# An audio tower on one core: the first quarter's turning and attention's first six projections, placed inside the convolution's last four iterations

## The chip, the cores and the metric

The kernel runs on one core of a Trainium2 chip. The metric is the device time of one execution in microseconds (us). The core's engines run side by side and meet only in semaphores: TensorE (PE; its weight loads are listed as PEld), VectorE (DVE), ScalarE (ACT), GpSimd (POOL) and SyncE (SP), whose queue issues the DMAs of this kernel. Each engine takes its own instructions in order.

## The reference, cut to what matters

```python
# x: [16, 64, 2048]; the convolution tokenizer makes h: [16, 128, 1024]
h = conv1d(x, conv_in_w, stride=1, pad=3)                       # 64 -> 128 channels, 7 taps
h = gelu(groupnorm1(h, gn1_w, gn1_b))
h = conv1d(h, dw_w, stride=2, pad=2, groups=H) + dw_b           # depthwise, 5 taps
h = conv1d(h, pw_w)                                             # pointwise, 128 -> 128
h = gelu(groupnorm1(h, gn2_w, gn2_b))
# then, each on layernorm(h):
q, k, v = n @ Wq.T, n @ Wk.T, n @ Wv.T     # 32 query heads, 8 key/value heads of 128
q, k = rotate(q), rotate(k)                # rotary position: x*cos + rotate_half(x)*sin
out = softmax(q k^T / sqrt(128)) v         # 4 query heads per key head, rows of one sequence: 128
h = h + out @ Wo.T
# ... routed low-rank experts, autocorrelation by a Fourier transform, a second routed layer
```

The last three stages aren't touched by the change.

## The kernel before

**Convolution** (`conv_stage`). 16 batches go through a software pipeline of 20 iterations, `it` = 0 to 19. In iteration `it` the 7-tap convolution of batch `it` runs on TensorE (48 products of 512 columns in four chunks, `conv`, L502 to L518), its means are taken on VectorE one iteration later (`head(0, it-1)`), the first gelu and the depthwise taps two later (`taps(it-2)`, four instructions on VectorE, L463), the pointwise product three later (`pointwise(it-3)`, L543) with `head(1, it-3)` behind it, and the second gelu, which writes row block `it-4` of `h`, four later (ScalarE, L386). `middle(it)` and `tail(it-1)` on VectorE, with two tiny products `average` on TensorE (L535), turn both means and variances into scale and shift: `tail` is a chain of sixteen small dependent instructions, and its last (L452) releases ScalarE's gelus. The batches end at `it` = 15, so iterations 16 to 19 have no `conv`; `from_end(it)` is 5 for iteration 15, and 4, 3, 2, 1 for the last four.

**Turning the first quarter** (`QuarterRows`). Attention works on quarters of four batches. For the first quarter, VectorE takes statistics of `h` (`rows.stats`, L170) in iterations 16 and 17 and the coefficients (`rows.coefficients`, `keep`, L175 to L183) in iteration 18. ScalarE normalizes (L192) and TensorE transposes (L204) through two PSUM banks; ScalarE rounds the result to `x_hi` (L212) and VectorE takes the rest as `x_lo` (L220). Batch b's transposes wait until batch b-1's `x_lo` has left the banks. All transposes stand in iteration 19.

**Attention** (`attention_stage`). It opens with a block that primes 27 semaphores, then `first()` and a step with `att` false that only makes the projections of the first head group: six tiles j = 0 (key), 1 (value), 2 to 5 (queries). One tile is 24 products of 512 columns (L1014 to L1016: 8 of `w_hi` by `x_hi`, 8 of `w_hi` by `x_lo`, 8 of `w_lo` by `x_hi`). Its weights land in one of two staging buffers; ScalarE makes `w_hi` (`split_w`, L727), VectorE `w_lo` (`low_w`, L885). Key and query tiles are rotated by four VectorE instructions (`rope_out`, L844 to L852), the value tile is copied by ScalarE (`v_out`, L759) and transposed (`turn_v`, L1069). Two PSUM banks alternate between tiles, so tile j waits for the rotation of tile j-2. Then 32 full steps follow, with scores (L1024), exponentials (L743), values and output products (L1061), each beside the next head group's projections.

The weights w_o of the output product are loaded by `load_o`, two tiles in `first()`. `after(engine, sem, n)` waits for a count of n+1 (the priming adds one).

Of the kernel before, what the change touches and what calls it, by code (L numbers as in the profile page):

```python
# [120 lines left out]
VALUES = TILES - 1  # L121

# [15 lines left out]
class QuarterRows:  # L138
# [6 lines left out]
    def __init__(self, nc, ctx, h, ident):  # L145
# [19 lines left out]
        prime(nc, [self.norm, self.normed, self.turned, self.hi_done, self.lo_done])  # L165
# [58 lines left out]
def conv_stage(nc, h, ident, ones_mean, x, conv_w, dw_w, chan, pw_wT, rows, w_stage):  # L224
# [8 lines left out]
    with ExitStack() as ctx:  # L233
# [65 lines left out]
        with nc.Block() as block:  # L299

            @block.sync
            def _(sp_):
# [9 lines left out]
                def body(it, par, on):  # L312
# [43 lines left out]
            def _(act):  # L356
# [16 lines left out]
                def body(it, par, on):  # L373
# [22 lines left out]
                    if from_end(it) == 2:  # L396
                        rows.normalize(act, 0, 0)
                        rows.normalize(act, 0, 1)
                    if from_end(it) == 1:
# [3 lines left out]
                        rows.high(act, 0, cp, 3)  # L403
                    if on(0):
                        evacuate(it, par, 0)
                        evacuate(it, par, 1)
                steps(act, body)

            @block.vector
            def _(dve):  # L410
# [55 lines left out]

                def body(it, par, on):
                    if not early(it, 2):
                        tail(it - 1)
                    if on(1):  # L470
                        head(0, it - 1, [raw[1 - par][:, c // 2, c % 2 * BANK:(c % 2 + 1) * BANK] for c in range(NCH)])
                    if on(3):
                        dve.wait_ge(pw_done, it - 2)
                        head(1, it - 3, [pp[:, c, :] for c in range(2)])
                    if on(2):
                        taps(it - 2, par, (1, 2))
                    if from_end(it) == 4:
                        dve.wait_ge(gelu2, QB)
                        rows.stats(dve, 0, rows_link, 0)
                        rows.stats(dve, 0, rows_link, 1)  # L480
# [4 lines left out]
                    if from_end(it) == 3:  # L485
                        rows.stats(dve, 0, rows_link, 2)
                        rows.stats(dve, 0, rows_link, 3)
                    if from_end(it) == 2:
                        rows.coefficients(dve, rows_link)
                        rows.keep(dve, rows_link, rows.rstd[:, :], rows.shift[:, :])  # L490
# [3 lines left out]
                rows_link = Links(dve, rows.norm, 1)  # L494
                steps(dve, body)

            @block.tensor
            def _(pe):
# [47 lines left out]
                def body(it, par, on):  # L546
# [5 lines left out]
                    if from_end(it) == 1:  # L552
# [9 lines left out]
                steps(pe, body)  # L562


def attention_stage(nc, h, ident, w_o, rope, rows, w_stage, next_rstd, next_shift):
# [8 lines left out]
    ROPED = TILES - 1  # L574
    with ExitStack() as ctx:
        def sb(name, shape, dt=F32):
            return ctx.enter_context(nc.sbuf_tensor(name, shape, dt))

# [3 lines left out]
        def psum(name):  # L582
            return ctx.enter_context(nc.psum_tensor(name, [P, BANK], F32))

        x_hi, x_lo = rows.x_hi, rows.x_lo
        o_stage = [sb(f"at_ostage{i}", [P, L]) for i in range(2)]
# [1716 lines left out]
```

## Time and profile before

| | |
|---|---|
| median of 3 runs | 2864.49 us |
| lowest, highest | 2861.25, 2867.18 us |
| profiled execution | 2863.8 us |
| its span, first to last instruction | 2862.1 us |
| outside the span | 1.7 us |
| mean granted TensorE clock | 0.979 of full |

| span, us | what runs |
|---|---|
| 0 to 240 | setup and iterations 0 to 15 of the convolution |
| 240 to 293 | iterations 16 to 18 |
| 293 to 306 | iteration 19 with the turning |
| 308 to 348 | attention's six projections alone |
| 348 on | 32 attention steps, then the last stages |

The timeline gives start and length of an instruction, or of a run of like ones (x4 is four of them), with the idle time of the engine before it and what ended that in square brackets. A window's granted clock is a share of full speed, 1.00 being 2.4 GHz and 0.50 being 1.2 GHz.

### The profile page before, as it was taken

How to read it: one execution, taken by the hardware profiler on the slowest of the kernel's cores; microseconds unless marked ns; L12 is line 12 of the kernel's file. 1: busy time of each engine (PE TensorE's matmuls, PEld its weight loads, DVE VectorE, ACT ScalarE, POOL GpSimd, SP SyncE). 2: the span in 40 equal slices, each digit the busy share in tenths (PEclk: the TensorE clock that was granted, in tenths of full speed). 3: DMA queues.
4: the chain of work that ended last, by engine and by line, in shares of the span. 5: the costliest groups of instructions: out<-in, count | busy, mean ns of one | idle time of the engine just before them, and what ended most of it. 6: DMA issues, size and time to landing. Idle time of an engine off the chain costs nothing. (4 is left out here: it accounts for less than half of the span.)

```text
span 2862.1 us, 37184 instructions
## 1 busy us (share of the span) xinstructions
PE 2722.3 (95%) x13162; PEld 2265.1 (79%) x13162; DVE 1812.0 (63%) x3247; ACT 980.8 (34%) x2012; POOL 108.2 (4%) x65
## 2 busy tenths in 40 slices
PE   7994799999999999999999999999999997899999
PEld 6773688888878888887888888788888876688888
DVE  4887566666765666667766666776666665872221
ACT  3553333332343333334323333333333333542121
POOL 2110000000000000000000000000000000221110
PEclk9997899999999999999999999999999998999999
DMA  4330232222222232222222222122222224000000
GB/s 111 74 74 0 74 99 91 78 81 81 81 67 82 76 98 90 81 81 74 75 82 81 73 95 95 57 92 81 81 81 74 80 66 155 2 16 30 25 27 30
DMA packets 55327, 206.69 MB, mean 72 GB/s; under 512 B 6769, under 2 KB 7153, under 8 KB 53169
## 3 DMA queue, kind: packets, MB, share of 16 engines
q1 hardware_dynamic: 55216, 205.26, 22.6%
q8 instruction: 64, 1.05, 0.2%
q14 instruction: 47, 0.38, 0.0%
HBM read 196.85 MB, written 8.39 MB: 72 GB/s over the span
## 5 line engine op out<-in xcount | busy, mean ns | idle before, releaser
L1014 PE MATMUL at_proj<-qr_xhi,at_whi 128*128 128x512 f32 x1536 | 614.5, 400 | 12.4 <-DVE at_wlo L885 8.0
L1016 PE MATMUL at_proj<-qr_xhi,at_wlo 128*128 128x512 f32 x1536 | 600.7, 391 | 0.0
L1015 PE MATMUL at_proj<-qr_xlo,at_whi 128*128 128x512 f32 x1536 | 599.0, 390 | 0.0
L755 ACT CAST at_ohi<-at_ov 128x512 fp32r<-128x512 f32 x128 | 75.2, 587 | 846.3 <-PE at_ov L1043 846.3
L1014 PEld LDWEIGHTS at_proj<-qr_xhi,at_whi 128*128 128x128 f32 x1536 | 289.2, 188 | 69.2 <-DVE at_wlo L885 8.7
L1016 PEld LDWEIGHTS at_proj<-qr_xhi,at_wlo 128*128 128x128 f32 x1536 | 288.6, 188 | 63.5
L1015 PEld LDWEIGHTS at_proj<-qr_xlo,at_whi 128*128 128x128 f32 x1536 | 289.6, 189 | 56.3
L1061 PE MATMUL at_out<-at_wohi,at_ohi 128*128 128x512 f32 x1008 | 311.5, 390 | 4.0 <-DVE at_wolo L890 3.0
L1061 PE MATMUL at_out<-at_wolo,at_ohi 128*128 128x512 f32 x1008 | 311.2, 390 | 0.0
L1061 PE MATMUL at_out<-at_wohi,at_olo 128*128 128x512 f32 x1008 | 311.2, 390 | 0.0
L897 DVE TENSOR_TENSOR h<-h,at_out 128x1024 f32 (+1 forms) x126 | 152.9, 1213 | 209.8 <-PE at_out L1061 209.8
L881 DVE TENSOR_TENSOR at_olo<-at_ov,at_ohi 128x512 fp32r<-128x512 f32 x128 | 88.3, 690 | 272.4 <-ACT at_ohi L755 272.4
L885 DVE TENSOR_TENSOR at_wlo<-at_wstage,at_whi 128x1024 fp32r<-128x1024 f32 x192 | 234.3, 1220 | 7.1 <-DMA at_cs<-in_rope_dram 5.4
L1061 PEld LDWEIGHTS at_out<-at_wohi,at_ohi 128*128 128x128 f32 x1008 | 189.7, 188 | 43.9 <-issue 3.3
L1061 PEld LDWEIGHTS at_out<-at_wolo,at_ohi 128*128 128x128 f32 x1008 | 189.8, 188 | 39.6
L1061 PEld LDWEIGHTS at_out<-at_wohi,at_olo 128*128 128x128 f32 x1008 | 189.8, 188 | 39.5
L727 ACT CAST at_whi<-at_wstage 128x1024 fp32r<-128x1024 f32 x192 | 203.0, 1058 | 42.0 <-PE at_proj L1016 39.1
L743 ACT ACTIVATE at_probs<-at_sc,at_ntop 128x128 f32<-128x128 f32 x512 | 181.5, 367 | 102.0 <-DVE at_ntop L859 101.6
L890 DVE TENSOR_TENSOR at_wolo<-at_ostage,at_wohi 128x1024 fp32r<-128x1024 f32 x128 | 153.6, 1221 | 1.4 <-ACT at_wohi L733 1.4
L733 ACT CAST at_wohi<-at_ostage 128x1024 fp32r<-128x1024 f32 x128 | 131.7, 1057 | 36.8 <-DMA at_ostage<-in_w_o_dram 36.5
L844 DVE TENSOR_TENSOR at_q<-at_proj,at_cs 128x512 f32<-128x512 f32 x128 | 88.1, 688 | 84.3 <-PE at_proj L1016 83.8
L1024 PEld LDWEIGHTS at_sc<-at_k,at_q 128*128 128x128 f32 x1024 | 132.0, 192 | 7.9 <-issue 0.6
(245 smaller groups left out, 4066.3 us busy)
## 6 DMA issues: line engine op xcount, KB each, us to landing
at_wstage<-in_w_qkv_dram SPq DMA_DIRECT2D x192, 512.0 KB, 3.7
at_ostage<-in_w_o_dram SPq DMA_DIRECT2D x128, 512.0 KB, 4.4
cv_x<-in_x_dram SPq DMA_DIRECT2D x32, 512.0 KB, 6.5
out_dram<-h SPq DMA_DIRECT2D x16, 512.0 KB, 2.6
fn_w_lo_raw<-in_w_t_dram SPq DMA_DIRECT2D x8, 512.0 KB, 8.6
fn_qka_lo_raw<-in_qka_t_dram SPq DMA_DIRECT2D x5, 512.0 KB, 12.3
fn_w_lo_raw<-in_dft_fwd_dram SPq DMA_DIRECT2D x4, 512.0 KB, 8.1
shared_raw<-in_a_route_dram SPq DMA_DIRECT2D x1, 544.0 KB, 3.9
```

Of the source, the lines that this page charges most:

```text
L727: act.copy(w_hi[j % 2][:, :], w_stage.buffers[j % 2][:, :]).then_inc(whi_done, 1)
L733: act.copy(wo_hi[:, r, :], o_stage[r % 2][:, :]).then_inc(wohi_done, 1)
L743: last = act.activation(probs[:, r, :], sc[b % 2][:, r * P:(r + 1) * P], ACT.Exp, bias=ntop[:, r:r + 1], scale=SCALE, accum_out=total[:, r ...
L881: dve.tensor_tensor(o_lo[:, :], ov[:, :], o_hi[:, :].bitcast(F32), ALU.subtract).then_inc(olo_done, 1)
L885: dve.tensor_tensor(w_lo[j % 2][:, :], w_stage.buffers[j % 2][:, :], w_hi[j % 2][:, :].bitcast(F32), ALU.subtract).then_inc(wlo_done, 1)
L890: dve.tensor_tensor(wo_lo[:, r, :], o_stage[r % 2][:, :], wo_hi[:, r, :].bitcast(F32), ALU.subtract).then_inc(wolo_done, 1)
L897: dve.tensor_tensor(hb, hb, part, ALU.add).then_inc(added, 1)
L1014: pe.matmul(proj[:, j % 2, :], hi[:, w], x_hi[:, k, :], start=(k == 0), stop=False)
L1015: pe.matmul(proj[:, j % 2, :], hi[:, w], x_lo[:, k, :], start=False, stop=False)
L1016: last = pe.matmul(proj[:, j % 2, :], lo[:, w], x_hi[:, k, :], start=False, stop=(k == KT - 1))
L1024: last = pe.matmul(sc[b % 2][:, r * P:(r + 1) * P], qT[par][:, r, cols], kT[par][:, cols], start=True, stop=True)
L1061: last = pe.matmul(banks[:, c, :], a[:, rows], w[:, r, c * BANK:(c + 1) * BANK], start=first, stop=end)
```

## The change

The statistics and coefficients of the first quarter move to the end of iteration 15, with the first two normalizations; the transposes, `high` and `low` move to iteration 16. The six projections with their splits and rotations stand in iterations 16 to 19 between the steps of the convolution, in a class `Projections` that attention also uses; attention loses its opening step. The first two weight tiles are loaded in iteration 0, ahead of the second input; further ones once the convolution's products are done, and the rotation table too. `w_o` is loaded in attention's `first()` as before, which now stands directly ahead of the first full step. The priming of 13 semaphores moves to SyncE's queue in iteration 0: the block of five in `QuarterRows` goes, and attention's block primes 18. `AttentionBuffers` gives attention's buffers the same places in both stages, over the convolution's input buffers.

SyncE's queue:

```diff
+                    if early(it, 1):
+                        for s in rows.sems + pro.sems:
+                            sp_.sem_inc(s, 1)
+                        w_stage.load(sp_, 0, 0)
+                        w_stage.load(sp_, 0, 1)
                 steps(sp_, body)
-                w_stage.load(sp_, 0, 0)
-                w_stage.load(sp_, 0, 1)
+                sp_.wait_ge(xlo_done, NB)
+                sp_.wait_ge(conv_done, NB * NCH)
+                pro.load_rope(sp_, rope)
+                for j in range(TILES + 1):
+                    after(sp_, pro.wlo_done, j + 1)
+                    w_stage.load(sp_, (j + 2) // TILES, (j + 2) % TILES)
```

ScalarE:

```diff
-                    if from_end(it) == 1:
+                    if from_end(it) == 4:
+                        act.wait_ge(xlo_done, NB)
+                        pro.split_w(act, 0, 0)
                         rows.high(act, 0, cp, 0)
                         rows.normalize(act, 0, 2)
...
-                    if from_end(it) == 2:
-                        rows.normalize(act, 0, 0)
-                        rows.normalize(act, 0, 1)
-                    if from_end(it) == 1:
+                    if from_end(it) == 4:
                         rows.high(act, 0, cp, 1)
                         rows.normalize(act, 0, 3)
                         rows.high(act, 0, cp, 2)
                         rows.high(act, 0, cp, 3)
+                        pro.split_w(act, 0, 1)
+                    if from_end(it) == 3:
+                        pro.split_w(act, 0, 2)
+                        pro.split_w(act, 0, 3)
+                    if from_end(it) == 2:
+                        pro.split_w(act, 0, 4)
+                        pro.split_w(act, 0, 5)
+                    if from_end(it) == 1:
+                        pro.split_w(act, 1, 0)
+                        pro.v_out(act, 0)
...
+                    if from_end(it) == 5:
+                        rows.normalize(act, 0, 0)
+                        rows.normalize(act, 0, 1)
```

VectorE:

```diff
+                    if from_end(it) == 5:
+                        dve.wait_ge(gelu2, QB)
+                        link = Links(dve, rows.norm, 1)
                         for b in range(QB):
-                            rows.low(dve, 0, cp, b)
+                            rows.stats(dve, 0, link, b)
+                        rows.coefficients(dve, link)
+                        rows.keep(dve, link, rows.rstd[:, :], rows.shift[:, :])
+
+                def ending(it, par, on):
+
+                    def last_16():
+                        tail(15)
+                        heads(16, 0, on, lambda: rows.low(dve, 0, cp, 0))
+                        dve.wait_ge(conv_done, NB * NCH)
+                        pro.low_w(dve, 0, 0)
+                        taps(14, 0, (1, 2))
+                        rows.low(dve, 0, cp, 1)
+                        middle(16)
+                        rows.low(dve, 0, cp, 2)
+                        rows.low(dve, 0, cp, 3)
+                        taps(14, 0, (3, 4))
+                        pro.low_w(dve, 0, 1)
+
+                    def last_17():
+                        tail(16)
+                        dve.wait_ge(pro.rope_in, 16)
+                        pro.rope_out(dve, 0, 0, 0)
+                        heads(17, 1, on, lambda: None)
+                        taps(15, 1, (1, 2))
+                        pro.low_w(dve, 0, 2)
+                        middle(17)
+                        taps(15, 1, (3, 4))
+                        pro.rope_out(dve, 0, 0, 1)
+                        pro.low_w(dve, 0, 3)
+
+                    def last_18():
+                        tail(17)
+                        pro.rope_out(dve, 0, 0, 2)
+                        pro.low_w(dve, 0, 4)
+                        heads(18, 0, on, lambda: None)
+                        pro.rope_out(dve, 0, 0, 3)
+                        pro.low_w(dve, 0, 5)
+                        middle(18)
+
+                    def last_19():
+                        tail(18)
+                        pro.rope_out(dve, 0, 0, 4)
+                        pro.low_w(dve, 1, 0)
```

TensorE:

```diff
-                    if from_end(it) == 1:
-                        pe.wait_ge(raw_done, NB * 2)
-                        for b in range(QB):
-                            rows.turn(pe, 0, cp, b)
...
+                def ending(it, par, on):
+
+                    def last_16():
+                        pe.wait_ge(raw_done, NB * 2)
+                        rows.turn(pe, 0, cp, 0, 1)
+                        pointwise(13, 1)
+                        average(16, on, 0)
+                        rows.turn(pe, 0, cp, 2)
+                        average(16, on, 1)
+                        rows.turn(pe, 0, cp, 3)
+                        pro.project(pe, 0, 0, 0)
+
+                    def last_17():
+                        pointwise(14, 0)
+                        pro.project(pe, 0, 0, 1)
+                        average(17, on, 0)
+                        average(17, on, 1)
+                        pro.project(pe, 0, 0, 2)
+
+                    def last_18():
+                        pro.project(pe, 0, 0, 3)
+                        pointwise(15, 1)
+                        pro.project(pe, 0, 0, 4)
+                        average(18, on, 0)
+                        average(18, on, 1)
+
+                    def last_19():
+                        pro.project(pe, 0, 0, 5)
+                        pe.wait_ge(gelu2, NB)
+                        pro.turn_v(pe, 0, ident)
```

`attention_stage`:

```diff
             first()
-            step(0, -1, 1, False, 2, False)
...
                 def first():
-                    sp.dma_start(cs[:, :, :], rope).then_inc(rope_in, 16)
                     load_o(0, 0, 0)
                     load_o(0, 0, 1)
-                    after(sp, wlo_done, 1)
-                    w_stage.load(sp, 0, 2)
```

`split_w`, `low_w`, `v_out`, `rope_out`, `project` and `turn_v` of `Projections` hold the same instructions and waits as the functions of `attention_stage` that they replace; `heads` is the two `head` calls with a place between them.

## Rows read from the trace of the kernel before

**Rows 1.** Page of the profile: TensorE's busy time, share of the span, instructions

```profile
PE 2722.3 (95%) x13162; PEld 2265.1 (79%) x13162; DVE 1812.0 (63%) x3247; ACT 980.8 (34%) x2012; POOL 108.2 (4%) x65
```

**Rows 2.** Windows by engine: start:end, length, busy (x) per engine, granted clock, DMA

```profile
238.50:262.00 23.50, 4.70 (x8) 1.97 (x8) 19.26 (x56) 5.24 (x5) 0.00 (x0) 0.64 0.00 0
...
292.00:307.00 15.00, 7.76 (x32) 6.12 (x32) 8.38 (x27) 10.23 (x13) 0.00 (x0) 0.50 0.00 1
```

**Rows 3.** Timeline, start and length in us, VectorE: iteration 16 of the convolution

```profile
240.02 0.16 DVE L447 TENSOR_SCALAR cv_var<-cv_sp 128x2 f32<-128x2 f32 x1
...
243.06 2.46 DVE L424 BATCH_NORM_STATS2 cv_st<-cv_raw 128x6 f32<-128x512 f32 x4
...
248.39 1.29 DVE L424 BATCH_NORM_STATS2 cv_st<-cv_pp 128x6 f32<-128x512 f32 x2 [2.56 <-PE cv_pp L543]
...
252.61 2.88 DVE L170 BATCH_NORM_STATS2 qr_st<-h 128x6 f32<-128x512 f32 x4
...
256.17 2.61 DVE L463 SCALAR_TENSOR_TENSOR cv_y<-cv_g,cv_dww,cv_y 128x1024 f32<-128x1024 f32 x2
```

**Rows 4.** Timeline: the coefficients' first instruction on VectorE, then ScalarE behind their last

```profile
288.57 0.20 DVE L176 BATCH_NORM_AGGREGATE qr_mv<-qr_st 128x2 f32<-128x12 f32 x1
...
292.40 2.37 ACT L192 ACTIVATE qr_xn<-h,qr_shift,qr_rstd 128x1024 f32<-128x1024 f32 x2 [10.51 <-DVE qr_shift L183]
```

**Rows 5.** Timeline, ScalarE and TensorE: iteration 16, with iteration 15's pointwise product first

```profile
230.45 1.95 PE L543 MATMUL cv_pp<-cv_y,cv_pw 128*128 128x512 f32 x4 [0.50 <-ACT h L386]
...
243.18 1.21 ACT L386 ACTIVATE h<-cv_pp,cv_shift,cv_scale 128x1024 f32<-128x1024 f32 x1 [3.90 <-DVE cv_shift L452]
...
244.29 2.08 ACT L391 ACTIVATE cv_g<-cv_raw,cv_shift,cv_scale 128x2048 f32<-128x2048 f32 x1
...
244.53 3.75 PE L543 MATMUL cv_pp<-cv_y,cv_pw 128*128 128x512 f32 x4 [6.18 <-ACT h L386]
```

**Rows 6.** Timeline: the turning stretch, its first instructions and its last

```profile
293.79 1.94 PE L204 MATMUL cv_cp<-ident,qr_xn 128*128 128x128 f32 x8 [4.82 <-ACT qr_xn L192]
...
295.53 0.69 DVE L220 TENSOR_TENSOR qr_xlo<-cv_cp,qr_xhi 128x512 fp32r<-128x512 f32 x1
...
305.11 0.69 DVE L220 TENSOR_TENSOR qr_xlo<-cv_cp,qr_xhi 128x512 fp32r<-128x512 f32 x1 [0.16 <-ACT qr_xhi L212]
```

**Rows 7.** Timeline: attention's start and the first two projections

```profile
307.92 1.99 ACT L727 CAST at_whi<-at_wstage 128x1024 fp32r<-128x1024 f32 x2 [2.85 <-PEq L81]
...
312.50 0.79 PE L1014 MATMUL at_proj<-qr_xhi,at_whi 128*128 128x512 f32 x1 [8.05 <-DVE at_wlo L885]
...
320.18 0.69 DVE L844 TENSOR_TENSOR at_k<-at_proj,at_cs 128x512 f32<-128x512 f32 x1 [6.61 <-PE at_proj L1016]
...
322.96 1.22 DVE L885 TENSOR_TENSOR at_wlo<-at_wstage,at_whi 128x1024 fp32r<-128x1024 f32 x1
...
325.62 0.69 DVE L844 TENSOR_TENSOR at_q<-at_proj,at_cs 128x512 f32<-128x512 f32 x1 [1.45 <-PE at_proj L1016]
```

**Rows 8.** Timeline: attention's first step behind the last of the six projections

```profile
347.99 1.28 ACT L764 ACT_TABLE_LOAD   x1
...
348.52 1.06 PE L1024 MATMUL at_sc<-at_k,at_q 128*128 128x128 f32 x8
...
353.84 2.00 ACT L733 CAST at_wohi<-at_ostage 128x1024 fp32r<-128x1024 f32 x2
```

**Rows 9.** Windows by engine, as rows 2: where the clock falls behind the convolution

```profile
240.00:242.00 2.00, 0.00 (x0) 0.00 (x0) 1.64 (x10) 0.00 (x0) 0.00 (x0) 0.88 0.02 4
```

**Rows 10.** Timeline: the convolution's start on GpSimd, ScalarE and TensorE

```profile
2.50 0.10 POOL L332 MEMSET cv_x<- 128x3 f32 x1 [1.01 <-POOLq L81]
...
17.87 1.13 ACT L364 CAST cv_xhi<-cv_x 128x1028 fp32r<-128x1028 f32 x1 [3.75 <-DMA cv_x<-in_x_dram]
...
27.95 0.39 PE L510 MATMUL cv_cp<-cv_xhi,cv_whi 128*128 128x512 f32 x1
```

**Rows 11.** DMA issues of the page: count, KB each, median us to landing

```profile
at_ostage<-in_w_o_dram SPq DMA_DIRECT2D x128, 512.0 KB, 4.4
```

More of the change, by code:

```diff
@@ L164, in __init__ @@
         self.hi_done, self.lo_done = sem("xhi_done"), sem("xlo_done")
-        prime(nc, [self.norm, self.normed, self.turned, self.hi_done, self.lo_done])
+        self.sems = [self.norm, self.normed, self.turned, self.hi_done, self.lo_done]
     def stats(self, dve, qt, link, b):
@@ L465, in taps, with heads @@
                                                       op0=ALU.mult, op1=ALU.add))
+                def heads(it, par, on, between):
+                    if on(1):
+                        head(0, it - 1, [raw[1 - par][:, c // 2, c % 2 * BANK:(c % 2 + 1) * BANK] for c in range(NCH)])
+                    between()
+                    if on(3):
+                        dve.wait_ge(pw_done, it - 2)
+                        head(1, it - 3, [pp[:, c, :] for c in range(2)])
                 def body(it, par, on):
@@ L469, in body @@
                         tail(it - 1)
[L470 to L474, printed above, removed]
+                    heads(it, par, on, lambda: None)
                     if on(2):
                         taps(it - 2, par, (1, 2))
[L477 to L480, printed above, removed]
                     if on(1) or on(3):
@@ L630, in steps @@
+        wlo_done = pro.wlo_done
+        tile_at = pro.tile_at
+        prime(nc, [wohi_done, wolo_done, ahead, vhi_done, vlo_done, sc_done, top_done, ntop_done,
+                   exp_done, rtotal_done, probs_done, pT_mm, phi_done, ov_mm, ohi_done, olo_done, out_mm, added])
         def steps(e, first, step):
             first()
-            step(0, -1, 1, False, 2, False)
             def quarter(qt, more):
@@ L722, in split_w @@
                 def split_w(s, j):
-                    act.wait_ge(w_stage.landed[j % 2], (s * (TILES // 2) + j // 2 + 1) * 16)
-                    if not (isinstance(s, int) and s == 0 and j < 2):
-                        after(act, proj_done, tile_at(s, j) - 1)
-                    act.copy(w_hi[j % 2][:, :], w_stage.buffers[j % 2][:, :]).then_inc(whi_done, 1)
+                    pro.split_w(act, s, j)
                 def split_o(s, r):
@@ L733, in split_o @@
                     act.copy(wo_hi[:, r, :], o_stage[r % 2][:, :]).then_inc(wohi_done, 1)
-                def first():
-                    split_w(0, 0)
                 def soft(n, b):
@@ L825, in step @@
                         rows.normalize(act, qt + 1, 1)
-                steps(act, first, step)
+                steps(act, lambda: None, step)
             @block.vector
@@ L830, in rope_out, with low_w @@
                 def rope_out(s, par, j):
[L832 to L852 removed]
+                    pro.rope_out(dve, s, par, j)
+                def low_w(s, j):
+                    pro.low_w(dve, s, j)
                 def top_of(n, b):
@@ L1063, in outputs @@
                     last.then_inc(out_mm, 1)
-                def turn_v(s):
-                    after(pe, vT_done, s + 1)
-                    after(pe, plo_done, s * QB)
-                    for b in range(QB):
-                        last = pe.transpose(tp[:, b * D:(b + 1) * D], vT[:, b * P:(b + 1) * P], ident[:, :])
-                    last.then_inc(v_turned, 1)
                 def step(qt, g, par, att, nxt, turn):
```

224 lines of the change are left out of this document (123 added, 101 removed).

## The prediction

> **What bounds the kernel now.** The page first [rows 1]: TensorE is busy for 95% of the span. So a change pays only where TensorE is idle or at half clock. The windows [rows 2] show such a place: in 238.5 to 262 TensorE is busy 4.70 of 23.5 us, and in 292 to 307 it is busy 7.76 of 15 us at a granted clock of 0.50, which is its 1.2 GHz level. The timeline says why. Iterations 16 to 18 have no convolution products, and VectorE's in-order chain sets the pace: tail, head, head, taps, middle, taps [rows 3]. Then the rows are turned [rows 6], attention's block starts, and six projections run with the other engines nearly idle [rows 7]. The path I follow is the stretch from 240.0 (first instruction of `tail(15)`, [rows 3]) to the first attention step, whose exponential table load stands at 347.99 and whose scores start at 348.52 [rows 8]. Before 240 and after 348 both kernels issue the same compute.
>
> **Prices.** From starts in the timeline: `tail` 243.06 - 240.02 = 3.04. `head(0)` 2.46 and an aggregate, 2.74. `head(1)` with its aggregate 1.58, of which 1.29 is the row. Two taps 2.61, with gap 2.65. Statistics of two batches 2.88; of four, 5.8. `middle`: 252.61 + 2.88 to 256.17, 0.68. All [rows 3]. Coefficients 292.40 - 288.57 = 3.83 [rows 4]. Pointwise 3.75 at half clock, 1.95 at full, and about 0.1 until VectorE reads it (248.39 - 244.53 = 3.86); the row-block gelu 1.1, the large gelu 2.08, the first tap 1.2 [rows 5]. Transposes of one batch 1.94 at half clock; 0.69 for each `low` [rows 6]. A projection 5.44 at full clock (325.62 - 320.18), 7.68 where it starts at half clock and the clock rises in it (320.18 - 312.50); a rotation 322.96 - 320.18 = 2.78; a `low_w` 1.22, a `split_w` 1.0 [rows 7].
>
> **The new order, station by station** (times in the clock of the trace of before; waits for several engines resolved by hand).
>
> Iteration 15: VectorE adds statistics and coefficients, 5.8 + 3.83, before `tail(15)`: 240.0 to 249.7. The same instructions are taken out of iterations 16, 17 and 18, so VectorE's total is unchanged; what is queued behind them is `tail(15)`, and behind that ScalarE's gelus. ScalarE normalizes two batches by 252.1; TensorE turns the first at 251.0 to 252.9, at half clock.
>
> Iteration 16: `tail(15)` to 252.7, `head(0,15)` to 255.5, `low` of batch 0 to 256.8. ScalarE: first split, two `high`, third normalization, then row block 12 by 256.5, large gelu, first tap by 259.8. TensorE turns batch 1 in 256.3 to 258.2, then pointwise(13), at half clock to 262.1; VectorE waits for it 5.3 us (2.56 before, [rows 3]), and this is the first cost of the change: the added wait is behind the second batch's transposes and the gelu that stands behind `high` and `normalize`. `head(1,13)` 263.7, `low_w` 264.9, taps 267.5, `low` of batch 1 268.9, `middle` 269.5. Batches 2 and 3 go through the two banks in turns. In iteration 19 four batches took 305.80 - 295.53 = 10.3 from first to last `low` [rows 6], one of them behind a gelu, so two cost 4.1 to 5.1; nothing stands between these, so 4.1: 270.1 to 274.2. Taps 276.9, second `low_w` 278.0. Projection 0 starts at 274.3 and takes 7.7 (cold start, as at 312.50): 282.0.
>
> Iteration 17: `tail(16)` 281.0. VectorE's next instruction is the key rotation, which waits for projection 0: 282.0 to 284.8; queued behind that wait are `head(1,14)` and batch 15's taps, and TensorE's averages wait for those. ScalarE's row block 13 is done at 282.2, pointwise(14) 282.4 to 284.4 at full clock, `head(1)` 286.4, taps 289.0, `low_w` 290.2. Projection 1 takes TensorE to 289.8, and `average` is queued behind it, so `middle` is at 291.1, taps 293.8, rotation 296.5, `low_w` 297.7. Projection 2: 291.7 to 297.1.
>
> Iteration 18: `tail` 300.7, rotation 303.5, `low_w` 304.7. Projection 3 waits for its `low_w`: 297.8 to 303.3; pointwise(15) 305.3; projection 4 305.4 to 310.8. `head(1,15)` 307.0, rotation 309.8, `low_w` 311.0, `middle` behind projection 4 and its average: 312.2.
>
> Iteration 19: the second average returns at 312.8, `tail` 315.9, rotation 318.6, `low_w(1,0)` 319.8. TensorE: projection 5 312.7 to 318.1, the value copy and its transposes to 319.7. The block ends at 319.8 instead of 305.80 (the last `low`, [rows 6]).
>
> Then attention's block: 305.80 to 307.92 was 2.1 us with 27 semaphores to prime [rows 6, 7]. It now primes 18; for five at the kernel's start the gap is 1.0 [rows 10]. By the line between these two, 1.7: the first step starts at 321.5. Its table load stood at 347.99, so 26.5 us are gained by ScalarE's path and 348.52 - 321.6 = 26.9 by TensorE's. In sum: 108.0 us become 81.5. What remains hidden is 5 x 5.44 of projection beside VectorE's chain; what isn't is the 14 us by which the chain grew.
>
> **The start.** The priming block of five goes: 1.0 us off everything behind it [rows 10]. Against it stand 13 increments and two 512 KB loads in SyncE's queue ahead of the second input. The trace doesn't show this; bounds: one such load lands 4.4 us after issue [rows 11], so the second input, split at 17.87, comes 0 to 8.8 later. Even at 26.7, with 1.13 for the split, it is ready at 27.8, and TensorE wants it at 27.95 [rows 10]; only ScalarE's evacuations queued behind that split slip, at most 0.9 on the path. I take 0, as the nearest row leaves slack. Increments lie between 0 and 0.05 each by the priming rows, hidden the same way.
>
> **The output weights.** `load_o` was issued 40 us ahead of use, now at the step's start. ScalarE's first use is 353.84 - 347.99 = 5.9 us into the step [rows 8]; the first lands at about 4.7, the second near 5.3 to 9.1 if they don't overlap [rows 11], wanted at 6.8. Cost 0 to 2.3; ScalarE has the first `values` split behind it, TensorE a whole projection. I take 0.
>
> **Sum.** 26.5 + 1.0 = 27.5. Against the profiled execution, 2863.8 (span 2862.1 and 1.7 outside): 2836.3. The median of the runs is 0.7 higher: 2837.0.
>
> **What a page says of it.** The clock stood at 0.50 through 32 transposes in 292 to 307 [rows 2]; the sum takes pointwise(13) behind eight transposes as cold. The Trainium skill (TensorE: Matmul & The Clock Gate, Part 4: PE-mode transpose) says that transposes don't count as busy time in the same way. By the page 262.1 stands; were they counted, the product would end 0.9 us sooner, by the cold start of the first projection, and the kernel would be at 2836.
>
> **Rivals.**
> 1. *The clock falls in the ending.* It fell in 240 to 242, TensorE's last convolution product lying just before 240 [rows 9]. TensorE's longest pause between projections is by my stations 1.9 us, with two tiny averages in it. If VectorE's chain is longer than I have it, pauses grow and single projections cost 10.5 (5.44 by the ratio of the pointwise rows, 3.75 / 1.95, [rows 5]) instead of 5.44: 5.0 each. One or two: 2842 to 2847. The same skill page has the rule this rests on (Why this matters for your kernels: avoid idle gaps between bursts); the trace has the fall.
> 2. *Slower than before.* All of TensorE's work between 274 and 320 at half clock. Walking the same stations with 10.5 for a projection and 3.75 for each pointwise: projections end at 284.8, 299.5, 312.0, 322.5, 336.8, 349.2, and the first step starts at 352.9, its first projection cold too (2.2): 352.9 - 348.0 - 1.0 + 2.2 = +6.1, 2870.6. It decides only when all six projections and both pointwise products are cold; with one of them warm the change still gains or stays even. Against it: the clock rose inside the first projection and stayed [rows 7].
> 3. *The work is serial anyway.* If pointwise, averages and projections wait in turns so that each projection's 5.44 lies wholly in VectorE's path, 5 x 5.44 = 27 comes back and the time is 2859 to 2864. Against it: the stations show VectorE idle only for only about 11 us between 256 and 313, and TensorE busy in most of them with work that was on its path before.
> 4. *More hidden than I count.* Projection 0 warm (2.2 less), the pointwise half warm (0.9), the priming dearer: 2831 to 2834.
>
> **How the numbers follow.** Forecast, 2835 to 2840: 0.55. Rival 4: 0.15. Rival 1: 0.15. The start or the output weights at their upper bounds (2838 to 2841): 0.05. Rival 3: 0.06. Rival 2: 0.04. For eight in ten: 2831 to 2847. A difference of 0.2%, 5.7 us, is about what can be told from no change here. Faster than 2858.8: the first four, 0.90. Within: most of rival 3, 0.06. Slower: 0.04.
>
> **What would show it.** After: the granted clock 1.00 in the windows from about 279 (278 with the earlier start) on; six projections at 5.4 but the first; VectorE's wait ahead of `head(1,13)` near 5 us and ahead of the key rotation near 1; scores at about 320.6. The prediction is wrong if a window between projections stands at 0.50, if VectorE's idle time in the ending is well over 11 us, or if the first step's output weights are waited for.

## The result, and the profile after

The changed kernel takes 2837.45 us in the median of 5 runs (2830.8 to 2843.4); the kernel before took 2864.49. The ratio is 0.9909, 95% interval 0.9896 to 0.9923: 27.0 us faster. The profiled execution took 2836.08 us, its span is 2834.3.

The page of the changed kernel: busy time of the engines, and the granted clock in 40 slices.

```profile
PE 2720.1 (96%) x13162; PEld 2265.8 (80%) x13162; DVE 1808.2 (64%) x3247; ACT 979.9 (35%) x2012; POOL 108.7 (4%) x65
...
PEclk9997999999999999999999999999999998999999
```

TensorE's busy time is the same as in [rows 1] within 2.2 us, and it makes as many products. So hardly any work went: of the 27.8 us by which the span is shorter, 25.6 are idle time of TensorE.

Windows of the changed kernel (columns as in [rows 2]): three in the convolution's ending, then the change to attention.

```profile
256.00:262.00 6.00, 4.68 (x10) 2.07 (x9) 1.28 (x2) 4.48 (x5) 0.00 (x0) 0.58 0.00 0
...
284.00:290.00 6.00, 4.60 (x23) 3.76 (x21) 5.75 (x13) 2.13 (x3) 0.00 (x0) 1.00 0.00 0
...
302.00:308.00 6.00, 6.00 (x24) 4.25 (x23) 5.17 (x10) 1.05 (x1) 0.00 (x0) 1.00 0.29 90
...
318.00:320.00 2.00, 0.00 (x0) 0.00 (x0) 0.00 (x0) 0.00 (x0) 0.00 (x0) 0.76 0.50 133
...
320.00:322.00 2.00, 1.21 (x5) 1.22 (x6) 0.00 (x0) 1.33 (x2) 0.00 (x0) 0.50 0.59 203
...
322.00:324.00 2.00, 2.00 (x9) 1.71 (x8) 1.40 (x3) 0.54 (x1) 0.00 (x0) 0.50 0.96 360
```

Where the kernel before stood at 0.50 to 0.64 [rows 2], the ending now runs at full clock from 280 to 318. The clock falls again between the stages, in 318 to 320, and stays at 0.50 in 320 to 324. The forecast did not have that; of the rivals only the second has a cold first projection, in a case where everything before it is cold too.

VectorE in the ending, timeline: statistics of four batches, the head behind pointwise(13), rotations 0 to 4, the last weight remainder, and attention's first instruction.

```profile
238.99 5.79 DVE L171 BATCH_NORM_STATS2 qr_st<-h 128x6 f32<-128x512 f32 x8
...
260.72 1.30 DVE L446 BATCH_NORM_STATS2 cv_st<-cv_pp 128x6 f32<-128x512 f32 x2 [4.94 <-PE cv_pp L604]
...
281.18 0.69 DVE L751 TENSOR_TENSOR at_k<-at_proj,at_cs 128x512 f32<-128x512 f32 x1 [1.54 <-PE at_proj L774]
...
292.59 0.69 DVE L751 TENSOR_TENSOR at_q<-at_proj,at_cs 128x512 f32<-128x512 f32 x1
...
299.53 0.69 DVE L751 TENSOR_TENSOR at_q<-at_proj,at_cs 128x512 f32<-128x512 f32 x1
...
305.75 0.69 DVE L751 TENSOR_TENSOR at_q<-at_proj,at_cs 128x512 f32<-128x512 f32 x1
...
313.98 0.69 DVE L751 TENSOR_TENSOR at_q<-at_proj,at_cs 128x512 f32<-128x512 f32 x1
...
316.75 1.22 DVE L729 TENSOR_TENSOR at_wlo<-at_wstage,at_whi 128x1024 fp32r<-128x1024 f32 x1
...
322.57 0.69 DVE L1027 TENSOR_TENSOR at_vlo<-at_tp,at_vhi 128x512 fp32r<-128x512 f32 x1 [4.60 <-ACT at_vhi L936]
```

The other engines: transposes, pointwise(13), projection 0, attention's table load, the first use of the output weights.

```profile
250.04 1.94 PE L205 MATMUL cv_cp<-ident,qr_xn 128*128 128x128 f32 x8 [12.71 <-ACT qr_xn L193]
...
257.06 3.62 PE L604 MATMUL cv_pp<-cv_y,cv_pw 128*128 128x512 f32 x4
...
272.99 0.77 PE L772 MATMUL at_proj<-qr_xhi,at_whi 128*128 128x512 f32 x1 [1.49 <-DVE qr_xlo L221]
...
320.66 1.28 ACT L936 ACT_TABLE_LOAD   x1 [3.62 <-PEq L81]
...
326.49 2.02 ACT L912 CAST at_wohi<-at_ostage 128x1024 fp32r<-128x1024 f32 x2
```

The stations stand nearly where the prediction put them, once its 1.0 us for the start is taken off: statistics 239.0 (238.99), head behind pointwise(13) 261.1 (260.72), key rotation 281.0 (281.18), rotation 1 292.8 (292.59), rotation 2 299.7 (299.53), rotation 3 306.0 (305.75), rotation 4 314.9 (313.98), last remainder's end 318.8 (317.97), table load 320.5 (320.66, against 347.99 in [rows 8]). VectorE's wait ahead of `head(1,13)` is 4.94 (5.3 forecast), ahead of the key rotation 1.54 (1.0). All its waits between 255 and 312 add up to 9.8 us, where the prediction had about 11 and called well over 11 a sign of being wrong.

To see where a lead is kept or lost I line up one instruction, VectorE's `v_low` (it writes `at_vlo`, the rest of the value tile), over the 32 attention steps. Lead over the first profile of the kernel before, in us, from starts that are known to 0.1:

```
                      step 0  step 1  step 7  step 8  step 16  step 24  step 31  end of span
changed kernel          27.3    25.8    25.8    23.9     22.2     22.1     22.2         27.8
changed, again (e4)     28.5    27.8    27.7    28.7     27.2     27.3     27.3         27.3
before, again (e10)     -0.4    -0.3    -0.4    -2.2     -3.9     -3.9     -3.9          1.7
turning alone (e1)       4.4     3.6     3.5     3.6      3.4      3.6      3.6          3.7
three hidden (e2)       19.1    17.2    17.1    16.6     14.2     13.8     13.8         13.7
start alone (e3)         2.7     2.8     2.7     1.0     -0.7      1.1      1.2          2.1
no priming block (e5)   27.9    27.2    27.1    24.9     23.6     23.7     23.7         23.7
pointwise first (e6)    31.4    30.7    30.6    28.7     26.8     26.7     26.7         26.5
both (e7)               32.2    32.3    32.2    32.3     32.1     32.1     32.2         32.2
loads later (e8)        27.0    25.5    25.4    23.5     21.2     21.2     21.2         21.3
last load out (e9)      28.3    28.4    28.3    26.6     26.1     26.5     26.5         32.1
```

All of the change's own effect is there at step 0. Within a quarter (steps 1 to 7, 8 to 15, and so on) every lead stands still within 0.4 us. It moves only in three places: the first step, the quarter turns ahead of steps 8, 16 and 24, and the last stages. What moves it there is the matter of e4 and e10.

### The profile page after: what moved, and what is told of

It reads as the page before. It is cut to its first block and busy times, and to the rows that moved or that the text cites. A ratio compares the mean times of both kernels' runs of the same rounds, so it can differ in the third digit from the quotient of the medians.

```text
span 2834.3 us, 37178 instructions
## 1 busy us (share of the span) xinstructions
PE 2720.1 (96%) x13162; PEld 2265.8 (80%) x13162; DVE 1808.2 (64%) x3247; ACT 979.9 (35%) x2012; POOL 108.7 (4%) x65
## 5 line engine op out<-in xcount | busy, mean ns | idle before, releaser
L1193 PE MATMUL at_out<-at_wohi,at_ohi 128*128 128x512 f32 x1008 | 311.2, 390 | 4.0 <-DVE at_wolo L1041 3.0
L1156 PE MATMUL at_sc<-at_k,at_q 128*128 128x128 f32 x1024 | 136.4, 277 | 3.7 <-PEq L81 3.0
```

What stands on the lines that cost most here:

```text
L1156: last = pe.matmul(sc[b % 2][:, r * P:(r + 1) * P], qT[par][:, r, cols], kT[par][:, cols], start=True, stop=True)
L1193: last = pe.matmul(banks[:, c, :], a[:, rows], w[:, r, c * BANK:(c + 1) * BANK], start=first, stop=end)
```

## The experiments

### e1: the turning moved, the projections not

```diff
                     def last_19():
                         tail(18)
-                        pro.rope_out(dve, 0, 0, 4)
+                        dve.wait_ge(pro.rope_in, 16)
+                        for j in range(4):
+                            pro.rope_out(dve, 0, 0, j)
+                            pro.low_w(dve, 0, j + 2)
+                        pro.rope_out(dve, 0, 0, 4)
                         pro.low_w(dve, 1, 0)
...
-                        pro.project(pe, 0, 0, 5)
+                        for j in range(TILES):
+                            pro.project(pe, 0, 0, j)
```

The projections go from their places in iterations 16 to 18, the rotations and weight remainders from 17 and 18, and ScalarE's splits of tiles 2 to 5 stand in iteration 19 too.

> The changed kernel with the six projections, their rotations and the later weight splits taken out from between the steps of iterations 17 to 19 and put behind all of them; the turning stays in iteration 16. Theory (the gain is the projections hidden beside VectorE's chain; turning early buys nothing, since iteration 16 grows by what iteration 19 loses): by the stations of the prediction the last projection ends about 340 and the first attention step starts near 343 to 344, so about 5 us of the 27 remain: 2859 to 2860. Rival (the 13 us of turning that left iteration 19 are the larger part): 2850 or less.

Measured: 2860.48 us, ratio 0.9990 (0.9977 to 1.0003); lead at step 0 4.4 us. Timeline, TensorE's two pointwise products behind the turning and its first projection; ScalarE's table load.

```profile
281.63 3.75 PE L595 MATMUL cv_pp<-cv_y,cv_pw 128*128 128x512 f32 x4 [9.53 <-ACT h L398]
...
297.44 3.75 PE L595 MATMUL cv_pp<-cv_y,cv_pw 128*128 128x512 f32 x4 [6.54 <-ACT h L398]
...
304.64 0.77 PE L759 MATMUL at_proj<-qr_xhi,at_whi 128*128 128x512 f32 x1
...
343.57 1.28 ACT L923 ACT_TABLE_LOAD   x1 [2.98 <-PEq L81]
```

The first projection starts at 304.64, 7.9 us sooner than at 312.50 [rows 7], but the two pointwise products are at half clock again and nothing covers the projections. The table load at 343.57 and the median lie where the theory put them (343 to 344; 2859 to 2860). The rival falls: moving 13 us of turning out of iteration 19 leaves 4.4 us at step 0, and a ratio that can't be told from no change. Early turning is what makes the rest possible; it is not the gain.

### e2: three of the six projections hidden

```diff
-                        pro.project(pe, 0, 0, 3)
                         pointwise(15, 1)
-                        pro.project(pe, 0, 0, 4)
...
-                        pro.project(pe, 0, 0, 5)
+                        for j in range(3, TILES):
+                            pro.project(pe, 0, 0, j)
```

VectorE's rotation 3 and its last weight remainder of this head group, and ScalarE's split of tile 5, move to iteration 19 with them.

> The changed kernel with projections 3, 4 and 5 behind the convolution's last averages, 0 to 2 where the change has them. Theory: VectorE's chain is shortened where it no longer waits for projections 3 and 4, so three projections outside cost about 7 us, not 16: first attention step 7 us later, 2843 to 2845. Rival (each hidden projection is worth its 5.4 us): 2853.

Measured: 2849.12 us, ratio 0.9942 (0.9922 to 0.9961). The median lies between the two; the trace decides. Timeline of TensorE: pointwise(15), projection 3, attention's first scores.

```profile
300.27 3.75 PE L604 MATMUL cv_pp<-cv_y,cv_pw 128*128 128x512 f32 x4 [5.09 <-ACT h L398]
...
307.06 0.48 PE L771 MATMUL at_proj<-qr_xhi,at_whi 128*128 128x512 f32 x1
...
328.98 2.07 PE L1155 MATMUL at_sc<-at_k,at_q 128*128 128x128 f32 x8 [2.34 <-PEq L81]
```

The step-0 lead is 19.1 against 27.3, so three projections outside cost 8.2 us, not 16.3: the theory stands with 1.2 us more than it said. By the second profile of the changed kernel (e4, 28.5) it would be 9.4. A row can account for the rest. Without projection 3 TensorE is idle for 5.09 us, the clock has fallen, and pointwise(15) takes 3.75 instead of 1.88. The projections also kept the clock up for the products between them. Behind step 1 the profiled execution lost another 3.3 us, at the quarter turns (17.1 to 13.8); the median isn't taken apart by that.

### e3: the start alone

```diff
-        prime(nc, [self.norm, self.normed, self.turned, self.hi_done, self.lo_done])
+        self.sems = [self.norm, self.normed, self.turned, self.hi_done, self.lo_done]
...
+                    if early(it, 1):
+                        for s in rows.sems:
+                            sp_.sem_inc(s, 1)
+                        w_stage.load(sp_, 0, 0)
+                        w_stage.load(sp_, 0, 1)
                 steps(sp_, body)
-                w_stage.load(sp_, 0, 0)
-                w_stage.load(sp_, 0, 1)
```

> The kernel before with only the change's start: the block that primes five semaphores goes, they are incremented in SyncE's queue, and the first two weight tiles are loaded behind the first input. Theory: 1.0 us faster than before, visible as TensorE's second batch starting at 27.0 instead of 27.95; 2863.5. Rival (the weights ahead of the second input hold TensorE up): slower by up to 4 us, with TensorE idle before its second batch.

Measured: 2863.16 us, ratio 1.0003 (0.9991 to 1.0015). GpSimd's first instruction behind the setup, and the split of the second input:

```profile
1.96 0.10 POOL L335 MEMSET cv_x<- 128x3 f32 x1 [0.47 <-POOLq L98]
...
20.81 1.12 ACT L367 CAST cv_xhi<-cv_x 128x1028 fp32r<-128x1028 f32 x1 [7.09 <-DMA cv_x<-in_x_dram]
...
26.44 0.39 PE L513 MATMUL cv_cp<-cv_xhi,cv_whi 128*128 128x512 f32 x1
```

The last row is TensorE's first product of the second batch, the sign that was named. The same product in the unaltered kernel before, run again (e10):

```profile
26.99 0.39 PE L510 MATMUL cv_cp<-cv_xhi,cv_whi 128*128 128x512 f32 x1
```

The missing block shows as 0.54 us (1.96 against 2.50, [rows 10]), and the second input's split comes 2.9 us later than at 17.87, still ahead of its use. The second batch starts 1.5 us sooner than at 27.95, but e10 has it at 26.99 with no change at all, so that sign proves nothing. The expected 1.0 us isn't confirmed: 0.54 is all that the trace shows of it, and the runs can't tell it from nothing. The lead of 1.0 with which the changed kernel enters iteration 15's end is no proof either: the unaltered kernel before, run again (e10), came to the end of that iteration 1.06 us sooner than in its first profile.

### e4 and e10: both kernels again, unaltered

> The changed kernel, unaltered, once more. Theory: the granted clock in attention's quarter turns and in the last stages falls differently from execution to execution, so the lead over the kernel before at the 32 attention steps, which went 27.3, 25.8, 23.9, 22.2 and back to 27.8 at the end in the first profile, will have other values behind the first step; median 2834 to 2841. Rival (the loss of 3.5 us at the two quarter turns belongs to the change, by another order or place of buffers): the same losses at the same steps, within 0.3 us.

> The kernel before, unaltered, once more. Theory (the granted clock falls for different lengths in each execution where TensorE pauses: in the convolution's end, at the three quarter turns and in the last stages): seven iterations between turns take the same time as in the first profile within 0.1 us, while the stretches with a turn, 792.0 to 868.0 among them, and the last stages differ by up to 2 us each and up to 6 us together. Rival (they are fixed in one kernel): all stretches within 0.3 us.

Measured: e4 2840.51 us in the median of 4 runs, 2836.64 profiled. e10 2862.12 in one execution. Windows over the first quarter turn, the same stretch of code in four executions: before, changed, changed again, before again.

```profile
800.00:810.00 10.00, 7.47 (x35) 5.71 (x35) 6.74 (x10) 6.94 (x11) 0.00 (x0) 0.83 0.05 7
810.00:820.00 10.00, 10.00 (x50) 8.43 (x49) 7.20 (x9) 3.54 (x4) 0.00 (x0) 1.00 0.61 205
```

```profile
774.20:784.20 10.00, 6.99 (x32) 5.21 (x32) 7.54 (x10) 6.81 (x11) 0.00 (x0) 0.78 0.11 31
784.20:794.20 10.00, 10.00 (x41) 8.16 (x40) 4.94 (x6) 3.43 (x4) 0.00 (x0) 0.88 0.37 129
```

```profile
773.00:783.00 10.00, 7.05 (x39) 5.78 (x40) 7.00 (x9) 6.05 (x9) 0.00 (x0) 1.00 0.20 57
783.00:793.00 10.00, 10.00 (x49) 8.43 (x49) 7.87 (x11) 4.90 (x12) 0.00 (x0) 1.00 0.58 199
```

```profile
797.00:807.00 10.00, 4.83 (x33) 3.58 (x32) 6.24 (x12) 7.94 (x19) 0.00 (x0) 0.95 0.00 0
807.00:817.00 10.00, 10.00 (x33) 7.94 (x33) 4.94 (x6) 3.32 (x4) 0.00 (x0) 0.71 0.49 157
```

The clock in this turn falls to 0.83 for one window in the first profile of before, to 0.78 and 0.88 in two for the changed kernel, and to 0.95 and 0.71 in the second profile of before. In e4 it doesn't fall. By the step table the stretch from step 7 to step 8 takes 76.0 us in the kernel before and 77.8 in the same kernel again; 77.9 in the changed kernel and 75.0 in the same kernel again. The last stages take 510.9 us in before and 505.3 in before again. So the 3.6 us that the changed kernel loses at two turns and the 5.6 us it wins back in the last stages are not its own. Both rivals fall. The theory for e10 held for the seven steps between turns and for the turns (under 2 us each), but not for the last stages: 5.6 us, where up to 2 were expected.

The last stages, before and before again: a window of 22 us, then one VectorE instruction, the fifth of 16 like ones, and the GpSimd instruction beside it.

```profile
2352.00:2374.00 22.00, 13.38 (x46) 10.55 (x45) 11.33 (x19) 9.95 (x31) 0.00 (x0) 0.61 0.13 48
...
2449.23 2.64 DVE L1975 TENSOR_TENSOR shared_raw<-h 128x512 f32<-128x512 f32 x1
...
2448.98 2.34 POOL L1156 TENSOR_TENSOR fn_qka_lo<-fn_qka_lo_raw,fn_qka_hi 128x1024 fp32r<-128x1024 f32 x1 [10.12 <-ACT fn_qka_hi L1150]
```

```profile
2355.90:2377.90 22.00, 13.39 (x56) 10.83 (x55) 11.30 (x19) 10.46 (x32) 0.00 (x0) 0.77 0.16 48
...
2450.68 0.69 DVE L1975 TENSOR_TENSOR shared_raw<-h 128x512 f32<-128x512 f32 x1
...
2450.70 2.89 POOL L1156 TENSOR_TENSOR fn_qka_lo<-fn_qka_lo_raw,fn_qka_hi 128x1024 fp32r<-128x1024 f32 x1 [10.12 <-ACT fn_qka_hi L1150]
```

The clock is 0.61 in one and 0.77 in the other. But 2.0 of the 5.6 us don't stand on TensorE: the VectorE instruction takes 2.64 us where GpSimd began 0.25 us ahead of it, and 0.69 where GpSimd began 0.02 us behind it. It is short in the changed kernel's first profile, in e9 and in e10, the three executions that win 5.6 us in the last stages, and long (2.5 to 2.9 us) in the other nine. That a small shift in time, such as the clock's falls make, decides which of the two begins first is likely; no run shows it alone. The runs of the changed kernel spread as widely, from 2830.8 to 2843.4.

### e5: without attention's priming block

```diff
                 pro.load_rope(sp_, rope)
+                for s in pro.later:
+                    sp_.sem_inc(s, 1)
...
-        prime(nc, [wohi_done, wolo_done, ahead, vhi_done, vlo_done, sc_done, top_done, ntop_done,
-                   exp_done, rtotal_done, probs_done, pT_mm, phi_done, ov_mm, ohi_done, olo_done, out_mm, added])
```

> The changed kernel with attention's priming block taken out; its 18 semaphores are incremented in SyncE's queue behind the load of the rotation table. In the changed kernel 2.7 us lie between the last weight remainder of the convolution's block and attention's first instruction, and TensorE's clock falls there, which costs 1.5 us more in the first projection. Theory (two block changes and 18 increments make the gap): it shrinks to 1.2 to 1.6, the clock stays at 1.00, and the lead over the kernel before at the second attention step is 2.5 us larger than in the changed kernel. Rival (the gap is the engines' fetch of new code, and not the priming): gap at least 2.4, clock falls as before, no gain.

Measured: 2837.47 us, ratio 0.9901 (0.9885 to 0.9918). VectorE's last remainder and ScalarE's table load:

```profile
317.93 1.22 DVE L732 TENSOR_TENSOR at_wlo<-at_wstage,at_whi 128x1024 fp32r<-128x1024 f32 x1
...
320.07 1.28 ACT L930 ACT_TABLE_LOAD   x1 [1.86 <-PEq L300]
```

The gap is 320.07 - 319.15 = 0.9 us instead of 320.66 - 317.97 = 2.7: the priming block is 1.8 us of it, more than expected. The clock's part came out smaller. It still fell here, to 0.59 in 320 to 322, and the lead dropped by 0.7 from step 0 to step 1 instead of 1.5. Measured from the first transposes on, which takes the start's scatter out (250.04 and 251.14), step 1 comes 137.3 us later in the changed kernel and 134.8 in e5: 2.5 us, as expected. But the changed kernel run again (e4) needs 134.5 us for that stretch unaltered, so this sum shows nothing by itself. The gap does: it is 2.7 in both profiles of the changed kernel and 0.9 here and in e7. The median shows none of it. In the profiled execution the quarter turns took 3.5 us back (27.2 to 23.7), as they took 3.6 from the changed kernel; what the first profile of the changed kernel has more is the 5.6 us of the last stages.

### e6: pointwise(13) ahead of the second batch's transposes

```diff
-                        rows.turn(pe, 0, cp, 0, 1)
+                        rows.turn(pe, 0, cp, 0)
                         pointwise(13, 1)
+                        rows.turn(pe, 0, cp, 1)
```

On ScalarE the third normalization goes behind the first tap.

> The changed kernel with iteration 16 reordered: ScalarE writes row block 12 ahead of the third normalization, and TensorE makes pointwise(13) ahead of the second batch's transposes. Theory (VectorE's wait of 4.9 us ahead of head(1,13) is on the path, and comes from that order): pointwise(13) ends 2.7 to 3 us sooner and the first attention step starts 2.5 to 3 us sooner, wait 2 us. Rival (turning batch 1 later holds up the banks and VectorE's low of batch 1 instead): the wait moves there and the first step is where it was, within 0.5.

Measured: 2837.31 us, ratio 0.9910 (0.9893 to 0.9926). TensorE's pointwise(13) and VectorE's head behind it:

```profile
253.49 3.75 PE L604 MATMUL cv_pp<-cv_y,cv_pw 128*128 128x512 f32 x4 [2.19 <-ACT h L397]
...
257.28 1.30 DVE L446 BATCH_NORM_STATS2 cv_st<-cv_pp 128x6 f32<-128x512 f32 x2 [2.19 <-PE cv_pp L604]
```

VectorE waits 2.19 us instead of 4.94, and from the first transposes to step 0 it is 69.1 us instead of 72.5: 3.4 us gained, the wait didn't move elsewhere. The changed kernel run again (e4) has a wait of 3.69 and takes 70.6, for there the clock rose inside pointwise(13); against that execution 1.5 us are left. With pointwise(13) at half clock in both (3.62 to 3.75 us), 2.19 stands against 4.94 in the changed kernel's first profile, in e5 and in e8. So the prediction's first named cost was real and came from the order. The median is that of the changed kernel: four executions can't show 1.5 to 3.4 us where one kernel spreads over 12.6.

### e7: both edits

> The changed kernel with both edits, the priming block out and pointwise(13) first. Theory: the two gains add, 5 to 5.5 us at the second attention step against the changed kernel: median 2832. Rival (the clock's falls in attention's quarter turns and in the last stages decide what is left): gain at the second step as said, but a median anywhere in 2829 to 2839.

Measured: 2833.24 us in the median of 4 runs, ratio to before 0.9894 (0.9877 to 0.9910); profiled 2831.67. ScalarE's table load, and the window over the change of stage:

```profile
315.77 1.28 ACT L931 ACT_TABLE_LOAD   x1 [1.87 <-PEq L300]
...
314.00:316.00 2.00, 0.73 (x5) 0.53 (x5) 0.85 (x1) 0.23 (x1) 0.00 (x0) 1.00 0.11 20
```

The clock stays at 1.00 through the change, no lead is lost in the first step, and from the first transposes to step 1 it takes 130.5 us against 137.3. So the edits give 6.8 us there against the changed kernel's first profile, 1.3 to 1.8 more than the expected 5 to 5.5, and the clock no longer fell. Against its second (134.5) they give 4.0. The median is the lowest of all kernels that ran several times, 4.2 us under the changed one; the intervals overlap, so the traces show that advantage and the runs don't yet.

### e8: the two weight loads in iteration 2

> The changed kernel with its first two weight tiles loaded in iteration 2 instead of ahead of the second input. Theory (the two loads delay the second input, but into slack): the split of the second input comes at about 17 instead of 19.9, and TensorE's first product of batch 1 and everything behind it stay within 0.2 us. Rival (the loads ahead cost something at the start): TensorE's batch 1 starts up to 1 us sooner.

In one execution, 2842.62 us. ScalarE's splits of the first and second input:

```profile
12.31 1.12 ACT L375 CAST cv_xhi<-cv_x 128x1028 fp32r<-128x1028 f32 x1 [5.11 <-DMA cv_x<-in_x_dram]
...
17.14 1.14 ACT L375 CAST cv_xhi<-cv_x 128x1028 fp32r<-128x1028 f32 x1 [3.71 <-DMA cv_x<-in_x_dram]
```

The second split is at 17.14 instead of 19.91; TensorE's first product of batch 1 is at 27.26 against 27.00, and the first input's split was 0.21 later too, which is most of the 0.26. The loads ahead delay the second input by 2.8 us into slack, as the theory had it. The total is inside the scatter of the turns (25.5 to 21.3).

### e9: the last weight load out of the block

```diff
-                for j in range(TILES + 1):
+                for j in range(TILES):
...
                     load_o(0, 0, 1)
+                    after(sp, wlo_done, TILES + 1)
+                    w_stage.load(sp, 1, 2)
```

> The changed kernel with the last of the weight loads that close the convolution's block issued in attention's first() instead, behind the two w_o loads. Between the last weight remainder (end 317.97) and attention's first instruction (320.66) the changed kernel has 2.7 us, the kernel before 2.1 with more semaphores to prime. Theory (SyncE can issue that load only when the last remainder is done, and reaches the block's end 0.4 to 0.5 later than the others): the gap is 2.2 to 2.3. Rival (the gap has to do with TensorE's or ScalarE's end of block): 2.7 as before.

In one execution, 2831.81 us. VectorE's last remainder and ScalarE's table load:

```profile
316.21 1.22 DVE L729 TENSOR_TENSOR at_wlo<-at_wstage,at_whi 128x1024 fp32r<-128x1024 f32 x1
...
319.66 1.28 ACT L938 ACT_TABLE_LOAD   x1 [3.17 <-PEq L81]
```

The gap is 319.66 - 317.43 = 2.2 instead of 2.7. So, as the theory had it, SyncE's issue of that load was the last thing to reach the block's end. The clock stayed at 1.00 in the windows behind it, and the first step lost nothing; with one execution that can be chance.

## Why the prediction was right, step by step

**What bounds the kernel.** Right, and e1 and e2 show the mechanism by halves: turning early alone gives 4.4 us at step 0, three hidden projections 19.1, six 27.3 to 28.5. Rival 3, the serial one, falls by the same numbers.

**The stations in iterations 15 to 18.** Right within about 0.6 us each, up to the last, `middle` of iteration 18, which was put at 311.2 and ended at 310.4. VectorE's chain by hand, with an instruction's start-to-start time from the kernel before, was enough. Two small errors cancel inside: iteration 16 ran up to 0.6 us ahead of its stations, and projection 0 took 8.2 us instead of 7.7 (281.18 - 272.99). Pointwise(13) was put at 3.75 and took 3.62; e6 shows that 2.7 of the 4.9 us of wait behind it could have been had back.

**Iteration 19 and the change of stage.** The sum of two errors that cancel. The last remainder ended 0.8 sooner than the station said, the same 0.8 as at `middle` of iteration 18. The gap behind it was put at 1.7, on a line through the gaps with 27 and 5 semaphores, and measured 2.7. The line was wrong in both of its assumptions: the block costs 1.8 us by itself (e5), and SyncE's last load adds 0.46 (e9), a queue in which I had counted the loads but not when the last could be issued.

**The clock.** Rival 1 put its fall between projections; it held there, at 1.00 in every window from 280 to 318. It fell where the forecast had nothing, in the 3 us between the stages, with all engines idle, and projection 0 of the next head group ran its first third at half clock: 1.5 us. In e7 and e9, with a gap of 0.9 and 2.2 us, it stayed; in e5, with 0.9, it fell all the same, and in e4, with 2.7, it cost only 0.7. So the length of the gap alone doesn't settle it, and what does stays open.

**The start.** The 1.0 us isn't shown. The trace has 0.54 and e3 can't tell it from nothing. The bound of 0 for the second input was right in trace and in e8.

**The output weights.** Taken at 0, and 0: first use at 326.49, 5.8 us into the step against 5.9 before, with no wait listed ahead of it.

**The sum.** 26.5 us at the table load were forecast. Measured are 27.3; less what the changed kernel was ahead before the ending (1.0 us) or what the missing block shows (0.54), that is 26.3 to 26.8. From the end of iteration 15 to the table load the changed kernel takes 81.7 us and, run again, 79.7, where 81.5 were forecast; the kernel before takes 108.0 and 109.4. So the agreement within 0.2 is that of one execution, and the gain in the ending is 26.3 to 29.7 us. That the total is 27.0 and not 24 or 31 is partly luck too: behind step 1 single executions go from 4.2 us lost (e6, e8) to 3.7 won (e9) against the first profile of the kernel before.

**Transposes and the clock.** The forecast took pointwise(13) as cold. In the changed kernel it follows eight transposes and takes 3.62 us; in the same kernel again it takes 2.37, and the window 259 to 260 stands at 1.00. Timeline of e4:

```profile
256.06 1.94 PE L205 MATMUL cv_cp<-ident,qr_xn 128*128 128x128 f32 x8 [3.35 <-DVE qr_xlo L221]
...
257.80 2.37 PE L604 MATMUL cv_pp<-cv_y,cv_pw 128*128 128x512 f32 x4
```

The clock rose about 1 us after the first true product and 2.7 after the first transpose; in the first profile it rose 3.9 us after that product's start, at 261.0. The Trainium skill (TensorE: Matmul & The Clock Gate, Part 4: PE-mode transpose) says that transposes don't count as busy in the same way. The first profile agrees; one execution goes against a strict reading, while the 32 scattered transposes of [rows 2] never raised the clock. What a transpose counts for stays open.

## What to carry to other kernels

Moving a stage's preparation into the one before pays by what it lets another engine do beside the bound chain, not by the length of what is moved: measure the two apart, as e1 and e2 do. Walk the chain of the bound engine instruction by instruction, with the waits of in-order queues; then look at the seam between the stages, where every queue must be empty, the slowest of them being easily one that only issues DMAs. And line up one instruction over a loop before reading a total: a lead that moves only at pauses, and by other amounts when the same kernel runs again, isn't the change's. Compare an edit with more than one profile of the unaltered kernel: e5's 2.5 us were inside what e4 moved by itself.

## What the runs showed of the hardware that I had not expected

- The same kernel's granted clock falls for different lengths in the same pause: 1.00, or 0.78 and 0.88, in the same turn. Single executions of the changed kernel lie 12.6 us apart, more than twice the 5.7 us that I had set as what can be told.
- A block that does nothing but prime 18 semaphores costs 1.8 us between two stages (a gap of 2.7 us with it, 0.9 without, in e5 and e7).
- A VectorE instruction took 2.64 us instead of 0.69 beside one of GpSimd that had begun 0.25 us ahead of it (e10).
- The hidden projections shortened other work: with three of them gone, a pointwise product among them went from 1.88 to 3.75 us.
